# Twelve of sixteen gate rows through memory, and some products 512 columns wide, in a fused attention and expert layer

## The reference

```
q, k, v = split(x @ Wqkv + bqkv);  q -= mean(q);  k -= mean(k)
q2 = l2norm_row(q*q / (sum(q*q) + 1e-7));  k2 = l2norm_column(k*k / (sum(k*k) + 1e-7))
t2 = q2 @ (k2.T @ v) / sqrt(1024)
x1 = layernorm(x + (v + t2) @ Wln + bln)
sel = sigmoid(x1 @ expert_sel.T)                       # 16 experts
out_ffn = sum_e sel[:, e] * (relu(x1 @ keys[e]) @ values[e])   # 256 -> 128 -> 256
out = layernorm(x1 + out_ffn)
```

## Time and profile before

| | |
|---|---|
| median of three runs | 1024.11 us |
| the profiled execution, its own time | 1022.25 us |
| span of its trace, first to last instruction | 1020.5 us |
| mean granted TensorE clock | 0.997 of full |
| bytes read from and written to HBM | 37.18 and 23.07 MB |

### The profile page before, as it was taken

How to read it: one execution, slowest core, us unless ns; L and a number is a source line. 1 busy time by engine, 2 the same in 40 slices (tenths; PEclk the granted TensorE clock), 3 DMA queues, 4 the chain that set the end, 5 groups by cost and what they waited for, 6 DMA issues and landing times.

```text
span 1020.5 us, 21965 instructions
## 1 busy us (share of the span) xinstructions
PE 997.0 (98%) x8324; PEld 984.7 (96%) x8324; DVE 812.0 (80%) x1874; ACT 529.2 (52%) x1150; POOL 210.7 (21%) x267
## 2 busy tenths in 40 slices
PE   7899999999999999999999999999999999999997
PEld 6789999999999999999999999999999999999997
DVE  4889887889768887798877888788887888778555
ACT  4566645566345653566445664456544566354323
POOL 0021112212222122221222112122211212122221
PEclk9999999999999999999999999999999999999999
DMA  5032111211122011220121311112111221111001
GB/s 184 22 113 75 44 43 62 88 62 43 43 99 90 22 44 63 84 94 32 44 73 54 105 43 43 63 54 94 43 43 62 83 66 43 43 65 42 23 2 42
DMA packets 47981, 62.19 MB, mean 61 GB/s; under 512 B 4098, under 2 KB 34562, under 8 KB 47876
## 3 DMA queue, kind: packets, MB, share of 16 engines
q1 hardware_dynamic: 47876, 60.79, 17.8%
HBM read 37.18 MB, written 23.07 MB: 59 GB/s over the span
## 4 chain that ended last, share of the span: by engine, by line
PE 85%; DVE 7%; ACT 3%; issue 2%; DMA 1%; SPq 0%; POOL 0%; DVEq 0%; ACTq 0%; POOLq 0%
PE up_bank L1333 31%; PE down_bank L1333 31%; PE ring_bank L1333 9%; PE qk_bank L1333 7%; PE g_bank L1333 3%; DVE x1T_l L959 1%; DVE gated_l L1103 1%; ACT z L642 1%; DVE gated L1097 1%; PE ring_bank L1584 1%; PE g_bank L1379 1%; PE ring_bank L1585 1%; ACT gated_h L560 1%; DVE qk L862 1%; DMA sel_rows<-sel 0%
## 5 line engine op out<-in xcount | busy, mean ns | idle before, releaser
L546 POOL PARTITION_BROADCAST sel_all<-sel_rows x240 | 196.1, 822 | 682.7 <-DVE gated L1097 615.7
L560 ACT ACTIVATE gated_h<-gated 128x512 fp32r<-128x512 f32 x256 | 161.5, 631 | 298.0 <-DVE gated L1097 294.4
L1333 PE MATMUL up_bank<-x1T_h,keys_h 128*128 128x256 f32 x1024 | 286.3, 280 | 2.1 <-DVE keys_l L1084 2.1
L1333 PE MATMUL down_bank<-vals_h,gated_h 128*128 128x256 f32 x1024 | 287.1, 280 | 0.3
L1333 PE MATMUL down_bank<-vals_l,gated_h 128*128 128x256 f32 x1024 | 286.2, 280 | 0.0
L1333 PE MATMUL down_bank<-vals_h,gated_l 128*128 128x256 f32 x1024 | 286.2, 280 | 0.0
L1333 PE MATMUL up_bank<-x1T_l,keys_h 128*128 128x256 f32 x1024 | 286.2, 279 | 0.0
L1333 PE MATMUL up_bank<-x1T_h,keys_l 128*128 128x256 f32 x1024 | 286.2, 279 | 0.0
L1103 DVE TENSOR_TENSOR gated_l<-gated,gated_h 128x512 fp32r<-128x512 f32 x256 | 172.2, 673 | 47.6 <-ACT gated_h L560 47.1
L1097 DVE SCALAR_TENSOR_TENSOR gated<-up_bank,sel_all 128x512 f32<-128x512 f32 x256 | 176.0, 688 | 39.5 <-PE up_bank L1333 34.9
L1333 PEld LDWEIGHTS up_bank<-x1T_h,keys_h 128*128 128x128 f32 x1024 | 194.0, 189 | 2.3 <-DVE keys_l L1084 2.3
(11 more groups left out here) (257 smaller groups left out, 1697.5 us busy)
## 6 DMA issues: line engine op xcount, KB each, us to landing
out<-z SPq DMA_DIRECT2D x32, 256.0 KB, 2.4
x_raw<-in_x SPq DMA_DIRECT2D x15, 512.0 KB, 4.8
xT_raw<-in_xT SPq DMA_DIRECT2D x14, 512.0 KB, 4.3
parked_q<-w_room SPq DMA_DIRECT2D x14, 512.0 KB, 2.6
q<-parked_q SPq DMA_DIRECT2D x56, 128.0 KB, 3.1
parked_x<-w_room SPq DMA_DIRECT2D x14, 512.0 KB, 2.6
w_room<-parked_x SPq DMA_DIRECT2D x56, 128.0 KB, 3.1
w_room<-in_keys SPq DMA_DIRECT2D x4, 512.0 KB, 4.5
```

The costliest lines, as they stand in the source:

```text
L546: nc.gpsimd.partition_broadcast(sel_all[:, e % 2], row, P).then_inc(sel_spread, 1)
L560: return nc.scalar.activation(dst, src, ACT.Copy, **kw)
L1333: last = mm(dst, lhs, rhs, start=start and i == 0, stop=stop and i == n - 1, **kw)
```

## The change

Four things are changed.

1. *Rows.* Of each group's 16 rows, the first four (NEAR) are still spread by GpSimd. SP writes the other twelve to a DRAM room `sel_out` in one transfer and then reads each back to all 128 partitions (`partition_broadcast` of a DRAM row, 256 KB written into SBUF), three steps (AHEAD) before its gate. `sel_all` has four rooms instead of two; `sel_rows` one instead of three. VectorE's gate waits for GpSimd's count or for the semaphore of the room.
2. *Columns.* The projection QK is made with products of 512 columns instead of two halves of 256; so is the up product in steps 0, 3, 20, 21, 25 and 28 of each iteration.
3. *Plan.* QR 1 goes from step 27 to 25, XR 0 from 28 to 27, ZN 0 and 1 from 26 and 27 to 29 and 30, one bias sum on x from 30 to 27.
4. *Rooms.* The split of g (`gT`) shares its room with the parts of x instead of those of k2; the wait for the KV product moves with it. In the first batch other rooms are named.

```diff
-        25: [("XS", 3)], 26: [("ZN", 0)], 27: [("QR", 1), ("ZN", 1)], 28: [("XR", 0)], 30: [("LG", 0)],
+        25: [("QR", 1), ("XS", 3)], 27: [("XR", 0)], 29: [("ZN", 0)], 30: [("LG", 0), ("ZN", 1)],
...
-    bias_x={9: 0, 14: 1, 30: 2, 31: 3},
+    bias_x={9: 0, 14: 1, 27: 2, 31: 3},
...
+WHOLE_UP = (0, 3, 20, 21, 25, 28)
+SPREAD = 4
+AHEAD = 3
+NEAR = 4
...
-        gT_h, gT_l = k2_h, k2_l
+        gT_h, gT_l = x_h, x_l
...
             def move_rows(it, off, g):
...
+                grp = G * (it + off) + g
+                sp.wait_ge(sel_made, grp + 1)
+                at_least(sp, sel_spread, NEAR * grp)
+                sp.dma_start(sel_rows[0:P:32], sel[0:NEAR, :]).then_inc(rows_in, 16)
+                at_least(sp, gate_applied, E * (grp - 1))
+                sp.dma_start(sel_out[g, NEAR:E], sel[NEAR:E, :]).then_inc(sel_written, 16)
+
+            def spread_far(f):
+
+                grp, e = divmod(f, E)
+                sp.wait_ge(sel_written, 16 * (grp + 1))
+                at_least(sp, gate_applied, f - SPREAD + 1)
+                sp.dma_start(sel_all[:, f % SPREAD],
+                             sel_out[grp % G, e].partition_broadcast(P)).then_inc(spread_in[f % SPREAD], 16)
...
-                if s % E == LAST_ROWS_STEP and it < B:
-                    move_last_rows(G * it + s // E)
+                if step_exists(it, s + AHEAD) and (s + AHEAD) % E >= NEAR:
+                    spread_far(step_no(it, s + AHEAD))
...
+            def spread_near(grp):
+                for e in range(NEAR):
+
+                    at_least(pool, gate_applied, grp * E + e - SPREAD + 1)
...
+                    nc.gpsimd.partition_broadcast(sel_all[:, e], row, P).then_inc(sel_spread, 1)
...
+                    if i == 0:
+                        at_least(act, kv_projected, it)
                     copy(x_h[:], x_raw[:, 2 * i:2 * i + 2]).then_inc(x_hi, 1)
...
-                at_least(act, kv_projected, b - 1)
                 copy(k2_h[:, t % 2], k2[:, t % 2], scale=k_scale[:, t % 2:t % 2 + 1]).then_inc(k_hi, 1)
...
-                    dve.wait_ge(sel_spread, f + 1)
+                    if f % E < NEAR:
+                        dve.wait_ge(sel_spread, NEAR * (f // E) + f % E + 1)
+                    else:
+                        dve.wait_ge(spread_in[f % SPREAD], 16 * ((E // SPREAD - 1) * (f // E) + f % E // SPREAD))
...
-                                           in1=sel_all[:, s % 2], op0=ALU.max,
+                                           in1=sel_all[:, s % SPREAD], op0=ALU.max,
...
-                        for half_of in range(2):
-                            cols = slice(half_of * C, (half_of + 1) * C)
-                            last = product(qk_bank[:, cols],
-                                           [(both(xT_h, xT_l, ALL, h, m, slice(i * P, (i + 1) * P)),
-                                             both(wqk_h, wqk_l, ALL, m, cols)) for m in range(M)],
-                                           start=half_of == 0, skip_group_check=True)
-                        last.then_inc(qk_projected, 1)
+                        product(qk_bank[:], [(both(xT_h, xT_l, ALL, h, m, slice(i * P, (i + 1) * P)),
+                                              both(wqk_h, wqk_l, ALL, m, ALL)) for m in range(M)],
+                                start=True).then_inc(qk_projected, 1)
...
+                    if s in WHOLE_UP:
+                        product(up_bank[s % 2][:], [(both(keys_h, keys_l, ALL, e, m, ALL),
+                                                     both(x1T_h, x1T_l, ALL, g, m, ALL)) for m in range(M)],
+                                start=True).then_inc(up_made, 1)
+                    else:
```

More of the change, by code:

```diff
@@ L65 @@
 ROWS_STEP = 14
-ROW_ROOMS = 3
-LAST_ROWS_STEP = 4
+WHOLE_UP = (0, 3, 20, 21, 25, 28)
+SPREAD = 4
+AHEAD = 3
+NEAR = 4
 BLOCK = 32
@@ L157, in build_program @@
         sel = sb("sel", [E, GN])
-        sel_rows = sb("sel_rows", [P, ROW_ROOMS, GN])
-        sel_all = sb("sel_all", [P, 2, GN])
+        sel_rows = sb("sel_rows", [P, GN])
+        sel_all = sb("sel_all", [P, SPREAD, GN])
         gated = sb("gated", [P, GN])
@@ L257, in build_program @@
             "logits_made", "logits_low", "logits_summed", "sel_made"))
-        rows_in = [sem("rows_in%d" % j) for j in range(4)]
+        rows_in, sel_written = sem("rows_in"), sem("sel_written")
+        spread_in = [sem("spread_in%d" % j) for j in range(SPREAD)]
         sel_spread, up_made, gate_applied, gated_hi, gated_lo, down_made = map(sem, (
@@ L447, in move_rows @@
             def move_rows(it, off, g):
-                at_least(sp, sel_made, half(it + off, g))
-                at_least(sp, sel_spread, (it + off) * STEPS + g * E)
-                for j in range(ROW_ROOMS):
-                    sp.dma_start(sel_rows[0:P:32, j], sel[4 * j:4 * j + 4, :]).then_inc(rows_in[j], 16)
-            def move_last_rows(grp):
-                sp.wait_ge(sel_spread, grp * E + 4)
-                j = ROW_ROOMS
-                sp.dma_start(sel_rows[0:P:32, 0], sel[4 * j:4 * j + 4, :]).then_inc(rows_in[j], 16)
+                grp = G * (it + off) + g
[10 more added lines that the diff above has]
+                             sel_out[grp % G, e].partition_broadcast(P)).then_inc(spread_in[f % SPREAD], 16)
             def load_xT0(p):
@@ L551, in _ @@
             pool.wait_ge(spread_ready, 1)
-            spread_group(0)
+            spread_near(0)
             for grp in range(1, B * G):
-                spread_group(grp)
+                spread_near(grp)
         @block.scalar
@@ L692, in late @@
                         act.wait_ge(logits_made, half(b, a))
-                        for j in range(4):
-                            at_least(act, rows_in[j], b * (16 * G) + 16 * a)
-                        at_least(act, sel_spread, b * STEPS + a * E - (E - 1))
+                        at_least(act, rows_in, 16 * (G * b + a))
+                        at_least(act, sel_written, 16 * (G * b + a))
+                        at_least(act, sel_spread, NEAR * (G * b + a - 1) + 1)
                         copy(sel[:], ring_of(it, s, kind, a)[LOW:LOW + E, :]).then_inc(logits_low, 1)
@@ L1598, in step @@
                     at_least(pe, gate_applied, f - 1)
-                    for half_of in range(2):
-                        cols = slice(half_of * QUARTER, (half_of + 1) * QUARTER)
-                        last = product(up_bank[s % 2][:, cols],
-                                       [(both(keys_h, keys_l, ALL, e, m, ALL),
-                                         both(x1T_h, x1T_l, ALL, g, m, cols)) for m in range(M)],
-                                       start=half_of == 0, skip_group_check=True)
-                    last.then_inc(up_made, 1)
+                    if s in WHOLE_UP:
[3 more added lines that the diff above has]
+                    else:
+                        for half_of in range(2):
+                            cols = slice(half_of * QUARTER, (half_of + 1) * QUARTER)
+                            last = product(up_bank[s % 2][:, cols],
+                                           [(both(keys_h, keys_l, ALL, e, m, ALL),
+                                             both(x1T_h, x1T_l, ALL, g, m, cols)) for m in range(M)],
+                                           start=half_of == 0, skip_group_check=True)
+                        last.then_inc(up_made, 1)
                 layer1(it, s)
```

19 lines of the change are left out of this document (7 added, 12 removed).

## The result

| | before | after |
|---|---|---|
| median of 20 runs each, side by side | 1019.44 us | 1022.88 us |
| lowest and highest | 1014.51, 1024.67 | 1020.47, 1028.09 |
| the profiled execution, its own time and span | 1022.25, 1020.5 | 1020.83, 1019.0 |
| mean granted clock | 0.997 | 0.995 |

The ratio is 1.0039, 95% interval 1.0023 to 1.0055: by the measure of the forecast (0.5%) no change, and if anything a little slower. 1022.88 lies inside the range that I gave, 996 to 1026, but I had forecast 1008 against a median of 1024.11, and nothing of that gain came. I had put 0.75 on faster. The profiled executions alone would say 1.4 us faster. So I compare traces to find causes, and ratios for verdicts.

A forecast was written before the change was run, and what follows sets the result against it. TensorE, busy 98% of the span, was taken as the bound. Savings of 0.1 + 1.4 + 0.6 = 2.1 us per iteration over 7.5 iterations, 15.7 us, plus 0.5 once, gave 1007, as a median 1008; range 996 to 1026 us.

The forecast's parts named there:

- Wide products: QK and six up steps: 168 narrow products become 84 of 512 columns at 232.5 ns, 0.1 us less per iteration.
- rival C: Wide products in rows of six run at the bare 213 ns, giving 996 us; chance 0.07.
- The pace: Remaining narrow TensorE products: fast share rises from 0.23 to 0.6, 1.4 us less per iteration; ends +0.9 and -2.9.
- Rival B: TensorE's pace does not get better, wide products turning fast to slow as often; 1018 to 1025 us, chance 0.21.
- LG 0's wait: TensorE's wait for x1T_l before LG 0 goes as XR 0 moves to step 27; 0.6 us less per iteration.
- XR, QR and ZN: Moved pieces at steps 25 to 30: delays covered, counted 0; without the two-step lag's cover 1 us per iteration.
- Rows through memory: Twelve GpSimd broadcasts replaced by row transfers landing in time; counted 0, bounds 0 to 0.2 us less per iteration.
- rival D: Rows land late behind SP's turns at steps 7 and 20, TensorE waits at 14 places; 1036 to 1050 us, chance 0.14.
- The base: The profiled execution of before, 1022.25 us, from which all sums start; taken as 1.9 us below the three-run median, 1024.11.

The follow-up runs named there:

- the last plan: The changed kernel with XR 0 at step 28, ZN 0 at 26 and ZN 1 at 28 behind XR 0; median 1004.66 us, ratio to before 0.9858.
- both kernels of TensorE alone: Two probes, no part of the reference: rows of 42 narrow products with varied breaks, and unbroken rows of 96 with varied operands and loads; 120.0 ns per product in both.
- the first kernel of TensorE alone: Probe, no part of the reference: rows of 42 narrow products, broken 130 times by wide or small products or waits; 120.0 ns per narrow product.

## Why the prediction was wrong

*Wide products, -0.1 us per iteration*: right. 232.5 ns as taken, 0.5 us in six iterations; rival C (213) was wrong.

*The pace, -1.4 us*: right in mechanism, too small in size. Within the six iterations the share went from 0.24 to 0.87, where 0.23 and 0.6 stood, and the term came to 2.4 us, inside its ends. The 0.23 was partly luck: the stretches named for it, 138.5 us and 12, give 0.20 of 737. The forecast that more places to turn raise the share and stalls turn it back is what the count of breaks shows. What it did not have is that the share of before is drawn in each execution (0.29 and 0.17 of the whole trace). Rival B did not happen.

*LG 0's wait, -0.6 us*: gone as forecast, 0.6 us, but XR 0's move, which I gave as the reason, is not needed for it: it is gone with XR 0 at step 28 too.

*XR, QR and ZN, 0*: this is the step that failed. The prediction said that VectorE's wait "delays gate 28 ... by about 1 us, covered by the two-step lag", of the ZN pairs that "nothing waits for them soon", and "I count 0; without that cover 1 us per iteration". I found a cover for each and did not add them: both fall on the same lag within three steps, and neither cover was whole: alone XR and ZN make 3.6 and 7.2 us of stalls in six iterations more than the last plan has. Measured, TensorE's stalls grew by 11.6 us in six iterations, 1.9 us each, net of the LG 0 wait that left; with 0.6 for that, the moves cost 2.5 us per iteration, two and a half times the price that I gave them without cover. The working had two holes. I looked for who waits for ZN, when the question was what ZN stands in front of: ScalarE's copy of the logits and VectorE's gated_l(30). And the delay at gate 28, given as about 1 us, is 1.6 in the iteration shown and up to 3.5.

*Rows through memory, 0*: no harm, as forecast (3.8 us median and 6.7 at most to landing, where 3.3 was taken), so rival D did not happen. But the kernel with the rows alone is 0.6% faster, four times the upper bound of 0.2 us per iteration that I had allowed (0.6% of 1020 us over 7.5 iterations is 0.8). Its trace has this in the pace and not in fewer waits; whether it is the rows' doing is open.

*The base*: the profiled execution of before was 2.8 us above the median of 20 runs, which the sum carried along.

With what was measured, my own sum is 0.1 + 2.4 + 0.6 - 2.5 = 0.6 us per iteration, 3.3 us in six. I had counted 7.5 iterations, but start and end, where I expected a gain, lost 1.8 us: 1022.25 - 3.3 + 1.8 = 1020.8, which is the profiled execution of after. That the medians lie the other way, 1019.44 and 1022.88, is how these two executions stand among their own 20 runs; the range of after's is 8 us, and I can't assign it further.

## What to carry to other kernels

When several pieces are moved, write down for each which slack covers it, and add up those that name the same slack; here a lag of two steps covered one late engine nearly, and two not at all. A copy that a wait is blamed on need not be what to move: look first at what stands ahead of it on its engine. Ask of a moved piece what it now stands in front of on its engine, not only who waits for it. And when the base of a sum is one execution of a kernel whose pace is drawn anew each time, have the spread of the base in the range.

## What the hardware showed

TensorE ran 256-column products, each with its weight load, at three distances at one granted clock of 1.00: 113.4 and 117.8 ns in the whole kernels and 120.0 in both kernels of TensorE alone. The same code had the fast one in 0.17 or 0.29 of its products. In sixteen traces a group of 512-column products without a stall kept the fast pace in 756 of 757 cases and brought it back in 79 of 291. The Trainium skill, page "TensorE: Matmul & The Clock Gate", section "Back-to-back issue gap", gives N / 2.4 GHz plus 2.5 ns for a product by itself, by which I estimate 109 ns for 256 columns, and measured 131 ns at 512 columns for streams with weight loads; no trace of this case shows either (113.3 ns in the fast stretches, and 232.6 ns or, in settled rows of twelve, 227). Products of 2 columns, each with its weight load, start 111 to 112 ns apart in the first kernel of TensorE alone and behind the first of each eight in before and after, so hardly earlier than those of 256.
